# Projections as three one-pass products of split operands, values as a sixth strip, x-hat normalised on GpSimd

## The chip, the cores and the metric

One core of a Trainium2 chip. The metric is the device time of one launch in microseconds (us). The core's engines run side by side and meet through semaphores: TensorE (PE; its weight loads are shown apart as PEld), VectorE (DVE), ScalarE (ACT), GpSimd (POOL), and SyncE (SP), which issues most DMAs.

## The reference

x is 2 x 2048 tokens of 512 features. One block of attention with a memory term, then a feed-forward product in rounded float8:

```python
x = L0_attn_x
xh = layernorm(x)                                  # no scale, no shift
q = xh @ Wq.T; k = xh @ Wk.T; v = xh @ Wv.T        # 512, 128 and 128 columns
# 4 query groups x 8 heads of 16; 8 heads of keys and values
probs = softmax(einsum('bsqhd,bthd->bqhst', qh, kh) * scale)
a_dot = einsum('bqhst,bthd->bsqhd', probs, vh)
sigma_q = elu(q by groups of 128)
a_mem = sigma_q @ memory / (sigma_q @ memory_norm)
w = sigmoid(memory_weight)
x = x + a_dot * (1 - w) + a_mem * w
y = layernorm(x) / s, clipped and rounded to float8_e4m3, times s
return x + y @ (weight * weight_scale).T
```

## The kernel before

The program has a preparation and then 64 heads (8 chunks of 512 tokens x 8 heads; head n is chunk n // 8). The change touches the preparation, and a little of the step into the first head.

*Preparation.* It runs over 8 chunks of 512 tokens (NG). For each chunk x-hat is made and turned so that features lie on partitions: VectorE's `statistics` (L1077, bn_stats) and `mean_and_variance` (L1082), GpSimd's `rstd_of` (L546, L549: an addition and a power of -1/2 on 128 x 4), VectorE's `normalise` (L1089, four 128 x 512 operations from resid to xn), TensorE's `turn_xn` (L743: for each of four k, four fp32 transposes into a PSUM bank, two banks by turns), ScalarE's `copy_xnT` (L627). Then TensorE projects in five strips of 128 outputs by 512 tokens, four of queries and one of keys (`project`, L770: four fp32 products over k, into one of four PSUM banks by turns), and the values token by token (`project_v`, L782: 16 products with x-hat as the weights and 128 columns, all in one bank), which ScalarE copies into v_tiles (`copy_v`, L657).

*What becomes of a strip.* It is cut into three bf16 parts that sum to it: ScalarE's `first_part` (L633), VectorE's `rest` (L1205, in place in PSUM), ScalarE's `second_part` (L646), VectorE's `last_part` (L1113). Of queries, elu(q) goes to DRAM: ScalarE's Relu and Exp (`exp_neg`, L637 and L641), VectorE's `add_sigma` (L1193). GpSimd squares the first part (L579); TensorE sums squares by head (`query_norms` L751, `key_norms` L758, one product of an fp32r operand with ones); VectorE keeps the largest (`largest_norm`, L1117). Keys are also summed (`sum_keys`, L1199). A bank is free for the strip four further on when its last part is written (part3_ready).

*The guard.* From the norms of a batch (chunks 0 to 3, 4 to 7) VectorE computes a bound on the scores (`guard_sums` to `fill_guard_rows`, L1143 to L1187), in chunk 4 for the first batch and behind chunk 7 for the second; if it is too wide, a slow path is taken (it isn't here). For the second batch the chain is VectorE, TensorE (L762), VectorE, GpSimd's root (L554), VectorE, TensorE's transpose (L832), VectorE's maximum and comparison (L1260, L1262), and a register load on TensorE.

*Order.* Each engine's program is written out by hand, in the order in which it works; nothing plans it. In a chunk TensorE has strips 0 to 4 (the key norms of the chunk before after strip 0), turns k = 0, 1 of the next chunk, query norms, values, turns k = 2, 3. VectorE, for each strip o: add_sigma(o), rest(o), last_part(o - 1), with the normalisation of the next chunk after strip 2, then statistics two chunks on. ScalarE, for each strip: first_part, exp_neg, second_part(o - 1). GpSimd: the squares, and rstd before strip 2's. SyncE stores 4 sigma strips and 15 parts a chunk, loads x two chunks on, stores v, in chunks 5 and behind 7 the guard's rows too, and in chunk 6 loads the first head's operands.

*Heads.* Head 0 begins when TensorE has scored two units (`score_early_units`, L850) and ScalarE exponentiates them (L707); TensorE weighs the values (L910). 64 heads follow.

Of the kernel before, what the change touches and what calls it, by code (L numbers as in the profile page):

```python
# [77 lines left out]

EXP_UNIT = 4 * math.log(2)
# [22 lines left out]
def attention_ffn(nc, x, Wq, Wk, Wv, memory, memory_norm, memory_weight, weight, weight_scale, input_scale, out,  # L102
# [5 lines left out]
    with ExitStack() as ctx:  # L108
# [13 lines left out]
        head_ones_r = sb("head_ones_r", [P, P], F32R)  # L122
# [6 lines left out]
        wT_ffn = sb("wT_ffn", [P, KT, DM], BF16)  # L129
# [7 lines left out]
        pool = sb("pool", [P, 8192], F32)  # L137
        probs = pool[:, 0:RING * QG * CH].rearrange("p (a b) -> p a b", a=RING)
        late_probs = pool[:, RING * QG * CH:(RING + 1) * QG * CH]
        by_token = sb("by_token", [P, QG, TPC, VW], F32)  # L140
        rden = sb("rden", [P, QG, TPC], F32)
        head_out = sb("head_out", [P, QG, TPC, DH], F32)

        xnT = pool[:, 0:4096].rearrange("p (a k s) -> p a k s", a=2, k=KT)
        xn = pool[:, 4096:6144].rearrange("p (t d) -> p t d", t=TPC)

        wqT = sb("wqT", [P, KT, DM], F32)
        wkT = sb("wkT", [P, KT, KV], F32)
        wvT = sb("wvT", [P, KT, KV], F32)
# [3 lines left out]
        k_sq = sb("k_sq", [P, CH], F32R)  # L153
        v_tiles = sb("v_tiles", [P, 2, HEADS, TPC, VW], F32)

        work = sb("work", [P, 8, CH], F32)
        late = work[:, :, :].rearrange("p a s -> p (a s)")
        late_x, late_z, late_p = (late[:, i * LATE * CH:(i + 1) * LATE * CH] for i in range(3))
        tile_work = [parts[:, :, :, :].rearrange("p o i s -> p (o i s)")[:, i * 2 * CH:(i + 1) * 2 * CH].bitcast(F32) for i in range(3)]
        neg, epos = work[:, 0:2, :], work[:, 2:4, :]  # L160
# [3 lines left out]
        sigma_st = wqT[:, 0, :]  # L164
# [3 lines left out]
        w_val = sb("w_val", [P, KT, DM], BF16)  # L168
        xqT = sb("xqT", [P, KT, P], BF16)
        xq_now = sb("xq_now", [P, DM], BF16)  # L170

        last_probs = pool[:, 0:RING * QG * CH].rearrange("p (a x q s) -> p a x q s", a=LAST_RING, x=2, q=QG)
        last_by_token = by_token[:, :, :, :].rearrange("p q t v -> p (q t v)").rearrange("p (t q v) -> p t q v", t=TPC, q=QG)
        last_xqT = pool[:, 0:TPC * KT * P // 2].bitcast(BF16).rearrange("p (t k s) -> p t k s", t=TPC, k=KT)
# [19 lines left out]
        gm_space = wkT[:, :, :].rearrange("p k o -> p (k o)").bitcast(BF16)[0:QG * TPC, :]  # L194
# [5 lines left out]
        pj = [ps[:, i, :] for i in (2, 3, 5, 6)]  # L200
# [10 lines left out]
        v_bank = [vp] * (NG - 2) + [tp[1], vp]  # L211
# [21 lines left out]
        w_copied = sem("w_copied")  # L233
        dec = sem("dec")
# [9 lines left out]
        xnT_ready = sem("xnT_ready")  # L244
# [13 lines left out]
        v_proj_ready = sem("v_proj_ready")  # L258
# [56 lines left out]
        def _(sp):  # L315
# [32 lines left out]
            def store_parts(c, par):  # L348
# [9 lines left out]
                for o in range(QG + 1):  # L358
# [15 lines left out]
                    if c == NG - 1 and o == QG - 1:  # L374
                        sp.wait_ge(sigma_stored[0], 32)
                        sp.wait_ge(proj_ready, c * (QG + 1) + QG)
                        load_sigma(0)
                if c < NG - 2:
                    store_v(c, par)
                elif c == NG - 1:  # L380
                    store_v(NG - 2, 1 - par)
                    store_v(NG - 1, par)
# [67 lines left out]
            for par in range(2):  # L450
                sp.wait_ge(v_stored[par], 16 * (NG // 2 + 1))
# [23 lines left out]


# [42 lines left out]
        def _(pool_e):  # L519
# [31 lines left out]

            def bound_roots(b):
# [28 lines left out]
            pool_e.tensor_tensor(head_ones_r[:, :], head_ones[:, :], head_ones[:, :], ALU.mult)  # L581
# [17 lines left out]
        def _(act):  # L599
# [4 lines left out]
            act.sem_inc(xnT_ready, TWO_FREE)  # L604
# [17 lines left out]
            def copy_xnT(c, par, ks, first=False):  # L622
                if not first:
                    act.wait_ge(v_proj_ready, c)
# [842 lines left out]
```

## Time and profile before

| | us |
|---|---|
| median of 3 runs | 2044.28 (2043.74 to 2045.47) |
| the profiled execution, its own time | 2043.78 |
| its span, first to last instruction | 2042.1 |
| first strip of chunk 1 starts | 37.48 |
| first strip of chunk 7 starts | 172.52 |
| first exponential of head 0 in the chain | 201.38 |

The span is what the trace covers, and the execution's own time has 1.7 us around it. The preparation is the first tenth of the span. A row of the chain of waits gives when a piece starts, how long it holds the chain, and what it is; records of instructions in a timeline start a little earlier than in the chain and overlap, since matmuls are pipelined, so lengths of runs of matmuls are read from the chain. The granted TensorE clock is 1.00 in every stretch of the preparation, the full 2.4 GHz.

### The profile page before, as it was taken

The numbers are of one execution on the slowest core, as the hardware profiler recorded it, in microseconds if no ns is written. First come the engines' busy times: TensorE is split into PE (matmuls) and PEld (weight loads), VectorE is DVE, ScalarE is ACT, GpSimd is POOL, SyncE is SP. The second block draws the span as 40 slices with busy tenths as digits, with TensorE's granted clock in tenths as the row PEclk, the third lists the DMA queues.
The fourth block names the chain that finished last, engine by engine and source line by source line (L and its number), as shares of the span: only waits on it lengthen the run. The fifth ranks groups of instructions, "written<-read, shape, count | busy, mean of one in ns | idle before, by whom it ended". The sixth has DMA issues, their size and how long they took to land.

```text
span 2042.1 us, 63426 instructions
## 1 busy us (share of the span) xinstructions
PE 2029.6 (99%) x27795; PEld 900.6 (44%) x27796; DVE 1110.6 (54%) x1721; ACT 1934.1 (95%) x2183; POOL 79.7 (4%) x139
## 2 busy tenths in 40 slices
PE   9999999999999999999999999999999999999998
PEld 5555434444444444444444444444444444444445
DVE  5775555455545555455554555545554555545555
ACT  5555999999999999999999999999999999999997
POOL 3222000000000000000000000000000000000000
PEclk9999999999999999999999999999999999999999
DMA  5665311111211211112121211111121211121111
GB/s 199 197 195 170 90 49 49 39 34 49 51 51 35 67 51 52 48 44 55 50 51 41 61 51 51 51 53 43 49 51 51 57 45 51 51 68 30 49 50 46
DMA packets 137687, 131.68 MB, mean 64 GB/s; under 512 B 31619, under 2 KB 113947, under 8 KB 137435
## 3 DMA queue, kind: packets, MB, share of 16 engines
q1 hardware_dynamic: 136571, 126.25, 22.2%
q8 instruction: 219, 3.59, 0.8%
q10 hardware_dynamic: 864, 1.57, 0.2%
q14 instruction: 33, 0.27, 0.0%
HBM read 86.57 MB, written 37.49 MB: 61 GB/s over the span
## 4 chain that ended last, share of the span: by engine, by line
PE 98%; DVE 1%; DMA 0%; ACT 0%; issue 0%; ACTq 0%; POOL 0%; DVEq 0%
PE ps L850 43%; PE ps L910 43%; PE ps L770 7%; PE ps L950 1%; PE ps L782 1%; PE ps L934 1%; PE ps L743 1%; PE ps L1003 1%; PE ps L1020 1%; DMA y_out<-in_Wq 0%; PE ps L732 0%; PE ps L751 0%; PE ps L758 0%; ACT pool L707 0%; ACTq L601 0%
## 5 line engine op out<-in xcount | busy, mean ns | idle before, releaser
L707 ACT ACTIVATE pool<-ps 128x1024 f32<-128x1024 f32 x1953 | 1794.9, 1155 | 3.4 <-PE ps L850 0.7
L850 PE MATMUL ps<-q_st,k_st 99*32 99x512 bf16 x16128 | 1100.4, 379 | 0.8 <-PE ps L850 0.4
L910 PE MATMUL ps<-pool,v_st 128*32 128x512 f32 (+1 forms) x8568 | 1061.2, 567 | 0.0
L850 PEld LDWEIGHTS ps<-q_st,k_st 99*32 99x32 bf16 x16128 | 446.5, 96 | 805.2 <-issue 495.0
L910 PEld LDWEIGHTS ps<-pool,v_st 128*32 128x32 f32 x8568 | 273.8, 110 | 205.2
L1311 DVE STREAM_TRANSPOSE by_token<-ps 128x512 f32<-128x512 f32 x63 | 45.2, 717 | 476.7 <-PE ps L910 476.7
L1304 DVE SCALAR_TENSOR_TENSOR work<-work 128x1024 f32<-128x1024 f32 x189 | 231.5, 1225 | 6.5
L1290 DVE TENSOR_SCALAR work<-ps 128x512 f32<-128x512 f32 x126 | 87.1, 692 | 127.9 <-PE ps L850 127.9
L770 PE MATMUL ps<-pool,wqT 128*128 128x512 f32 x256 | 113.6, 594 | 0.4 <-ACT pool L627 0.3
L1367 DVE SCALAR_TENSOR_TENSOR y_out<-ps,scalars,resid 128x512 f32 (+1 forms) x28 | 21.0, 750 | 112.7 <-PE ps L934 112.7
L1295 DVE SCALAR_TENSOR_TENSOR work<-work 128x1024 f32<-128x1024 f32 x63 | 77.2, 1226 | 2.2
L1306 DVE SCALAR_TENSOR_TENSOR pool<-work 128x1024 f32<-128x1024 f32 x63 | 77.2, 1225 | 2.2
L633 ACT ACTIVATE parts<-ps 128x512 bf16<-128x512 f32 x40 | 23.9, 597 | 56.5 <-PE ps L770 56.5
L592 POOL TENSOR_TENSOR var_eps<-moments,eps 128x1 f32<-128x1 f32 x32 | 6.1, 190 | 1810.2 <-DVE moments L1340 1810.2
L1301 DVE SCALAR_TENSOR_TENSOR work<-work 128x1024 f32<-128x1024 f32 x63 | 76.7, 1217 | 0.0
L770 PEld LDWEIGHTS ps<-pool,wqT 128*128 128x128 f32 x256 | 47.4, 190 | 54.5 <-issue 51.5
L1193 DVE SCALAR_TENSOR_TENSOR y_out<-work,ps 128x512 f32<-128x512 f32 x32 | 21.9, 683 | 48.8 <-ACT work L641 48.8
L1378 DVE SCALAR_TENSOR_TENSOR resid<-ps,rnorm,resid 128x128 f32 (+1 forms) x128 | 39.0, 346 | 15.1 <-DVE rnorm L1374 14.6
L1299 DVE TENSOR_SCALAR work<-work 128x1024 int32<-128x1024 int32 x63 | 43.7, 694 | 2.2
L1292 DVE TENSOR_SCALAR work<-work 128x1024 f32<-128x1024 f32 x63 | 43.7, 694 | 2.1
L934 PE MATMUL ps<-wT_ffn,xqT 128*32 128x512 bf16 x448 | 44.5, 380 | 0.0
L950 PE MATMUL ps<-mem_aug,wqT 128*32 128x129 f32 x1024 | 39.7, 273 | 0.0
(131 smaller groups left out, 842.8 us busy)
## 6 DMA issues: line engine op xcount, KB each, us to landing
q_st<-q_aug SPq DMA_DIRECT2D x384, 64.0 KB
v_st<-v_aug SPq DMA_DIRECT2D x64, 256.0 KB
q_aug<-parts SPq DMA_DIRECT2D x96, 128.0 KB
k_st<-k_aug SPq DMA_DIRECT2D x64, 192.0 KB
sigma_kept<-y_out SPq DMA_DIRECT2D x32, 256.0 KB, 3.9
k_st<-k_aug SPq DMA_DIRECT2D x64, 128.0 KB
wqT<-sigma_kept SPq DMA_DIRECT2D x32, 256.0 KB, 3.2
resid<-in_x SPq DMA_DIRECT2D x7, 1024.0 KB, 9.0
```

The lines of the kernel that those rows point to most:

```text
L707: act.activation(held[:, half_u * 2 * CH:half_u * 2 * CH + 2 * CH], sc[unit % SLOTS].rearrange("p a b -> p (a b)"), ACT.Exp, scale=EXP_UNIT)\
L770: last = pe.matmul(pj[i % len(pj)], w, xnT[:, par, k, :], start=(k == 0), stop=(k == KT - 1))
L850: last = pe.matmul(dst[VW * c:VW * c + VW, :], k_st[0:AUG, par, keys:keys + VW], q_st[0:AUG, par, q * CH:q * CH + CH], start=True, stop=True)
L910: last = pe.matmul(acc[par][VW * c:VW * c + VW, :].rearrange("v (i s) -> v i s", s=VW)[:, places, :], v_st[:, par, j, :], by_place[:, c, p ...
L934: last = pe.matmul(ffn_ps[VW * c:VW * c + VW, :], xqT[:, k, VW * c:VW * c + VW], wT_ffn[:, k, :], start=(k == 0), stop=(k == KT - 1))
L950: last = pe.matmul(am[VW * c:VW * c + VW, t, :], sigma_st[:, tokens:tokens + VW], mem_aug[:, :], start=True, stop=True)
L1290: dve.tensor_scalar(late_x[:, d * CH:d * CH + CH], acc[1 - par], LOWEST, None, ALU.max).then_inc(late_taken, 1)
L1295: dve.scalar_tensor_tensor(late_x, late_z, ROUND, late_x, ALU.subtract, ALU.subtract).then_inc(late_step, 1)
L1301: dve.scalar_tensor_tensor(late_p, late_x, POWER[4], late_x, ALU.add, ALU.mult).then_inc(late_step, 1)
L1304: dve.scalar_tensor_tensor(late_p, late_p, POWER[i], late_x, ALU.add, ALU.mult).then_inc(late_step, 1)
L1306: dve.scalar_tensor_tensor(late_probs[:, LATE * CH:2 * LATE * CH], late_p, POWER[0], late_z, ALU.add, ALU.mult)\
L1311: dve.transpose(by_token[:, :, :, :].rearrange("p q t v -> p (q t v)"), acc[par]).then_inc(acc_read, 1)
```

## The change

The operands of the projections are each written as two fp32r tiles, a high part (what a ScalarE copy into fp32r keeps) and a low part (VectorE: the turned value less the high part). Each fp32 product over k becomes three one-pass products: high weight by high x-hat, low weight by high x-hat, high weight by low x-hat (PASSES). The same splitting is done once for the turned weights (`split_weight`), which lie in other PSUM banks than before (WEIGHT_BANK).

The values are projected like a query strip, as strip 5 of the chunk, into the ring of four banks; ScalarE copies them to v_turn (`take_v`), and TensorE turns them back by tokens with four transposes (`turn_v`) behind the first strip of the next chunk; `copy_v` follows there. For chunk 7 the turning stands behind the two early units of head 0 and its copy behind ScalarE's second exponential. Chunk 6's and chunk 7's value strips both stand in the last chunk, as before.

The normalisation of chunks 1 to 7 moves from VectorE to GpSimd, before the squares of the chunk ahead of it; that of chunk 0 stays on VectorE. TensorE turns k = 0, 1 of the next chunk behind strip 2 and k = 2, 3 behind strip 3 (in chunk 0 behind strips 3 and 4). The turning of k = 2 waits until the low part of k = 0 is written, since both use one bank. The squares of keys are bf16 rather than fp32r. SyncE stores a chunk's values one chunk later. Tiles of the preparation and of the heads share space by the order of allocation.

```diff
+PASSES = ((0, 0), (1, 0), (0, 1))
+V_STRIP = QG + 1
+STRIPS = [(c, o) for c in range(NG) for o in range(QG + 1 + (c < NG - 2))] + [(NG - 2, V_STRIP), (NG - 1, V_STRIP)]
+STRIP_NUMBER = {co: s for s, co in enumerate(STRIPS)}
+WEIGHT_BANK = (5, 4, 2, 3, 0, 1)
+FIRST_TURN_BANK = (6, 7, 0, 1)
+LAST_V_AT = 1
+TURN_AFTER = (3, 2)
...
+            x_high = early("x_high", [P, 2, KT, CH], F32R)
+            x_low = early("x_low", [P, 2, KT, CH], F32R)
+            xn = early("xn", [P, TPC, DM], F32)
...
+            wq_low = early("wq_low", [P, KT, DM], F32R)
+            wk_low = early("wk_low", [P, KT, KV], F32R)
+            wv_low = early("wv_low", [P, KT, KV], F32R)
+            v_turn = early("v_turn", [P, CH], F32)
...
+        def bank(c, o):
+            return pj[STRIP_NUMBER[c, o] % len(pj)]
+
+        def turn_bank(c, k):
+            return ps[:, FIRST_TURN_BANK[k], :] if c == 0 else tp[k % 2]
+
+        v_bank = [vp] * (NG - 1) + [n2]
...
+                    if o == 0 and 0 < c < NG - 1:
+                        store_v(c - 1, 1 - par)
+                if c == NG - 1:
                     store_v(NG - 2, 1 - par)
-                    store_v(NG - 1, par)
...
+            def normalise(c, par):
+                pool_e.wait_ge(rstd_ready, c + 1)
+                pool_e.wait_ge(tp_ready, c * KT)
+                for t in range(TPC):
+                    last = pool_e.tensor_scalar(xn[:, t, :], resid[:, c * TPC + t, :], moments[:, par, t, 0:1],
+                                                rstd[:, par, t:t + 1], ALU.subtract, ALU.mult)
+                last.then_inc(xn_ready, 1)
...
-                    if o == 2 and not last:
-                        pool_e.wait_ge(sq_ready, c * (QG + 1) + o)
+                    if o == 0 and not last:
                         rstd_of(c + 1, 1 - par)
-                        pool_e.wait_ge(rstd_ready, c + 2)
+                        normalise(c + 1, 1 - par)
...
+            def copy_x_high(c, par, ks):
+                if c >= 2:
+                    act.wait_ge(proj_ready, STRIP_NUMBER[c - 2, V_STRIP] + 1)
                 for k in ks:
                     act.wait_ge(tp_ready, c * KT + k + 1)
-                    act.activation(xnT[:, par, k, :], tp[k % 2], ACT.Copy).then_inc(xnT_ready, 1)
+                    act.activation(x_high[:, par, k, :], turn_bank(c, k), ACT.Copy).then_inc(x_high_ready, 1)
...
+            def take_v(c):
+                act.wait_ge(proj_ready, STRIP_NUMBER[c, V_STRIP] + 1)
+                act.wait_ge(v_turned, c)
+                act.activation(v_turn[:, :], bank(c, V_STRIP), ACT.Copy).then_inc(v_taken, 1)
...
                         second_part(c, o - 1)
+                    elif c == 0:
+                        for j in (KT, KT + 1):
+                            copy_weight(j)
+                        act.wait_ge(small_loaded, 80)
+                        act.activation(e_neg, mem_w, ACT.Exp, scale=-1.0).then_inc(e_neg_ready, 1)
+                    else:
+                        copy_v(c - 1, 1 - par)
+                    if o == TURN_AFTER[c > 0]:
+                        copy_x_high(c + 1, 1 - par, range(KT // 2))
+                    elif o == TURN_AFTER[c > 0] + 1:
+                        copy_x_high(c + 1, 1 - par, range(KT // 2, KT))
+                second_part(c, QG)
                 if c < NG - 2:
...
+                    take_v(c)
...
+                    if unit == LAST_V_AT:
+                        copy_v(NG - 1, (NG - 1) % 2)
...
-                    pe.wait_ge(xnT_ready, c * KT + k + 1)
+                    if c > 0:
+                        pe.wait_ge(x_low_ready, c * KT + max(k - 1, 0))
                     for t in range(TPC):
-                        last = pe.transpose(tp[k % 2][:, t * P:t * P + P], xn[:, t, k * P:k * P + P], ident[:, :])
+                        last = pe.transpose(turn_bank(c, k)[:, t * P:t * P + P], xn[:, t, k * P:k * P + P], ident[:, :])
...
+            def product(c, par, o, k, p):
+                w_part, x_part = PASSES[p]
+                if o < QG:
+                    w = (wqT, wq_low)[w_part][:, k, o * P:o * P + P]
+                else:
+                    w = ((wkT, wk_low), (wvT, wv_low))[o - QG][w_part][:, k, :]
+                return pe.matmul(bank(c, o), w, (x_high, x_low)[x_part][:, par, k, :],
+                                 start=(k == 0 and p == 0), stop=(k == KT - 1 and p == len(PASSES) - 1))
+
+            def bank_free(c, o):
+                s = STRIP_NUMBER[c, o]
+                if s < len(pj):
+                    if s == 1:
+                        pe.wait_ge(x_low_ready, 1)
+                    return
+                held_c, held_o = STRIPS[s - len(pj)]
+                if held_o == V_STRIP:
+                    pe.wait_ge(v_taken, held_c + 1)
+                else:
+                    pe.wait_ge(part3_ready, held_c * (QG + 1) + held_o + 1)
+
+            def project(c, par, o, ks=range(KT)):
                 for k in ks:
-                    if o == 0:
-                        pe.wait_ge(xnT_ready, c * KT + k + 1 + TWO_FREE)
-                    w = wqT[:, k, o * P:o * P + P] if o < QG else wkT[:, k, :]
-                    last = pe.matmul(pj[i % len(pj)], w, xnT[:, par, k, :], start=(k == 0), stop=(k == KT - 1))
+                    for p in range(len(PASSES)):
...
+            def first_of_chunk(c, par):
                 for k in range(KT):
...
+                    pe.wait_ge(x_high_ready, c * KT + k + 1)
+                    for p in range(2):
+                        product(c, par, 0, k, p)
+                for k in range(KT):
+                    pe.wait_ge(x_low_ready, c * KT + k + 1)
+                    last = product(c, par, 0, k, 2)
+                last.then_inc(proj_ready, 1)
+
+            def turn_v(c):
+                pe.wait_ge(v_taken, c + 1)
+                if c < NG - 1:
+                    pe.wait_ge(v_tile_ready, c + ONE_FREE)
+                for t in range(TPC):
+                    last = pe.transpose(v_bank[c][:, t * P:t * P + P], v_turn[:, t * P:t * P + P], ident[:, :])
+                last.then_inc(v_turned, 1)
 
             def chunk(c, par, first_guard=False):
                 for o in range(QG + 1):
...
+                    bank_free(c, o)
+                    if c == 0:
+                        pe.wait_ge(w_split, o + 1)
+                    if o == 0:
+                        first_of_chunk(c, par)
+                    else:
+                        project(c, par, o)
+                    if o == 0:
+                        if c == 0:
+                            for j in (KT, KT + 1):
+                                turn_weight(j)
+                        else:
+                            key_norms(c - 1)
+                            turn_v(c - 1)
                     if first_guard and o == 2:
                         pe.wait_ge(v_tile_ready, c + 1)
                         mean_key_norm(0)
-                turn_xn(c + 1, range(KT // 2))
+                    if c == 0 and o == TURN_AFTER[0]:
+                        pe.wait_ge(w_split, KT + 2)
+                    if o == TURN_AFTER[c > 0]:
+                        turn_xn(c + 1, range(KT // 2))
+                    elif o == TURN_AFTER[c > 0] + 1:
+                        turn_xn(c + 1, range(KT // 2, KT))
                 query_norms(c)
-                if first_guard:
-                    pe.wait_ge(bound_in, 2)
                 if c < NG - 2:
-                    pe.wait_ge(v_tile_ready, c + 1)
-                    for t in range(TPC):
-                        project_v(c, par, t)
-                    turn_xn(c + 1, range(KT // 2, KT))
+                    bank_free(c, V_STRIP)
+                    if c == 0:
+                        pe.wait_ge(w_split, KT + 2)
+                    project(c, par, V_STRIP)
...
+            def split_weight(j):
+                dve.wait_ge(w_copied, j + 1)
+                turned = ps[:, WEIGHT_BANK[j], :]
+                if j < KT:
+                    high, low = (w[:, :, j * P:j * P + P] for w in (wqT, wq_low))
+                    dve.tensor_tensor(low, turned.rearrange("p (k o) -> p k o", k=KT), high.bitcast(F32), ALU.subtract)\
+                        .then_inc(w_split, 1)
+                else:
+                    high, low = (w[:, :, :].rearrange("p k o -> p (k o)") for w in ((wkT, wk_low), (wvT, wv_low))[j - KT])
+                    dve.scalar_tensor_tensor(low, turned, SCALE / EXP_UNIT if j == KT else 1.0, high.bitcast(F32),
+                                             ALU.mult, ALU.subtract).then_inc(w_split, 1)
+
+            def split_x(c, par, k):
+                dve.wait_ge(x_high_ready, c * KT + k + 1)
+                dve.tensor_tensor(x_low[:, par, k, :], turn_bank(c, k), x_high[:, par, k, :].bitcast(F32), ALU.subtract)\
+                    .then_inc(x_low_ready, 1)
 
             statistics(0)
             dve.wait_ge(stats_ready, 1)
             mean_and_variance(0)
...
+            split_weight(0)
+            normalise_first()
+            split_weight(1)
+            for k in range(KT // 2):
+                split_x(0, 0, k)
+            split_weight(2)
+            split_x(0, 0, 2)
+            split_weight(3)
+            split_x(0, 0, 3)
+            dve.wait_ge(x_loaded[1], 16)
+            statistics(1)
...
+                dve.wait_ge(stats_ready, c + 2)
+                mean_and_variance(1 - par)
                 for o in range(QG + 1):
+                    if o == TURN_AFTER[c > 0] + 1:
+                        for k in range(KT // 2):
+                            split_x(c + 1, 1 - par, k)
+                    elif o == TURN_AFTER[c > 0] + 2:
+                        for k in range(KT // 2, KT):
+                            split_x(c + 1, 1 - par, k)
                     if o < QG:
```

## Rows read from the trace of the kernel before

**Rows 1.** The page, busy time: us, share of the span, instructions.
```profile
PE 2029.6 (99%) x27795; PEld 900.6 (44%) x27796; DVE 1110.6 (54%) x1721; ACT 1934.1 (95%) x2183; POOL 79.7 (4%) x139
```
**Rows 2.** Busy time by stretch, chunk 1: stretch, length, engines' us (instructions), clock, DMA.
```profile
40.90:64.20 23.30, 23.30 (x95) 13.23 (x94) 15.81 (x29) 12.76 (x24) 6.40 (x7) 1.00 0.61 197
```
**Rows 3.** Chain of waits: start us, us, what (instructions).
```profile
37.48 3.44 PE ps L770 x8
...
41.14 13.73 PE ps L770 x32
54.88 0.87 PE ps L743 x8
55.75 0.33 PE ps L751 x4
56.08 3.77 PE ps L782 x32
...
60.72 3.44 PE ps L770 x8
64.16 0.24 PE ps L758
...
153.84 3.44 PE ps L770 x8
...
172.52 1.10 PE ps L770 x2
...
201.38 1.91 ACT pool L707 x2
```
**Rows 4.** Groups by shape, 0 to 170 us: busy us, mean ns | idle before.
```profile
L782 PEld LDWEIGHTS ps<-wvT,pool 128*128 128x128 f32 x192 | 21.9, 192 | 1.4 <-issue 1.4
L770 PEld LDWEIGHTS ps<-pool,wkT 128*128 128x128 f32 x55 | 10.4, 190 | 13.2 <-issue 13.2
L579 POOL TENSOR_TENSOR q_sq<-parts 128x512 bf16<-128x512 bf16 x28 | 29.3, 1045 | 83.2 <-ACT parts L633 82.6
L540 POOL MEMSET ones_row<- 128x512 bf16 x1 | 0.6, 550 | 0.0
```
**Rows 5.** Timeline of ScalarE in chunk 4, one strip: start us, us, instruction.
```profile
117.81 0.60 ACT L633 ACTIVATE parts<-ps 128x512 bf16<-128x512 f32 x1 [1.14 <-PE ps L770]
118.30 0.59 ACT L637 ACTIVATE work<-ps 128x512 f32<-128x512 f32 x1
118.98 0.63 ACT L641 ACTIVATE work<-work 128x512 f32<-128x512 f32 x1
119.52 0.58 ACT L646 ACTIVATE parts<-ps 128x512 bf16<-128x512 f32 x1
```
**Rows 6.** Timeline of VectorE in chunk 4.
```profile
116.21 0.69 DVE L1193 SCALAR_TENSOR_TENSOR y_out<-work,ps 128x512 f32<-128x512 f32 x1 [1.28 <-ACT work L641]
116.82 0.69 DVE L1205 TENSOR_TENSOR ps<-ps,parts 128x512 f32<-128x512 f32 x1
...
125.86 0.65 DVE L1160 TENSOR_TENSOR bound<-bound 128x1 f32<-128x1 f32 x1
...
128.58 0.68 DVE L1199 TENSOR_REDUCE k_sum<-ps 128x1 f32<-128x512 f32 x1
...
131.74 2.46 DVE L1077 BATCH_NORM_STATS2 stats<-resid 128x6 f32<-128x512 f32 x4
```
**Rows 7.** Timeline of GpSimd in chunk 4: the two steps of rstd.
```profile
118.53 0.20 POOL L546 TENSOR_TENSOR var_eps<-moments,eps 128x4 f32<-128x4 f32 x1 [2.44 <-DVE moments L1082]
118.81 1.01 POOL L549 TENSOR_TENSOR rstd<-var_eps,minus_half 128x4 f32<-128x4 f32 x1
```
**Rows 8.** Chain of waits in chunk 0, at the first turning of x-hat.
```profile
10.76 0.21 issue
10.97 0.64 PE ps L743 x4
```
**Rows 9.** Timeline of VectorE in chunk 0: its four normalisations, merged.
```profile
8.96 1.91 DVE L1089 TENSOR_SCALAR pool<-resid,moments,rstd 128x512 f32<-128x512 f32 x4 [1.42 <-POOL rstd L549]
```

More of the change, by code:

```diff
@@ L474, in _ @@
                 sp.wait_ge(gm_loaded, 16 * QK_LOADS * (NG * HEADS + 1) + 32)
+            store_v(NG - 1, 1)
+            for par in range(2):
+                sp.wait_ge(v_stored[par], 16 * (NG // 2 + 1))
             def load_block(g, h):
@@ L686, in last_chunk @@
                         second_part(c, o - 1)
+                take_v(c - 1)
+                second_part(c, QG)
                 copy_v(c - 1, 1 - par)
-                second_part(c, QG)
-                copy_v(c, par)
-            copy_xnT(0, 0, range(KT), first=True)
-            for j in (KT, KT + 1):
-                copy_weight(j)
-            act.wait_ge(small_loaded, 80)
-            act.activation(e_neg, mem_w, ACT.Exp, scale=-1.0).then_inc(e_neg_ready, 1)
+                take_v(c)
+            copy_x_high(0, 0, range(KT))
             for c in range(NG - 1):
@@ L766, in project @@
                 for k in ks:
-                    if o == 0:
-                        pe.wait_ge(xnT_ready, c * KT + k + 1 + TWO_FREE)
-                    w = wqT[:, k, o * P:o * P + P] if o < QG else wkT[:, k, :]
-                    last = pe.matmul(pj[i % len(pj)], w, xnT[:, par, k, :], start=(k == 0), stop=(k == KT - 1))
+                    for p in range(len(PASSES)):
+                        last = product(c, par, o, k, p)
                 if KT - 1 in ks:
                     last.then_inc(proj_ready, 1)
-            def project_and_turn(c, par):
-                for k in range(KT // 2):
-                    project(c, par, 0, range(k, k + 1))
-                    turn_xn(c, range(KT // 2 + k, KT // 2 + k + 1))
-                project(c, par, 0, range(KT // 2, KT))
@@ L833, in last_chunk @@
                 last.then_inc(ranges_ready, 1)
-                for t in range(1, TPC):
-                    project_v(c, par, t)
-            pe.wait_ge(w_copied, 2)
-            turn_xn(0, range(KT // 2))
-            pe.wait_ge(w_copied, KT)
-            project_and_turn(0, 0)
-            for j in (KT, KT + 1):
-                turn_weight(j)
+            turn_xn(0, range(KT))
             for c in range(NG - 1):
@@ L1112, in last_part @@
                 dve.wait_ge(part2_ready, i + 1)
[L1113 removed]
+                dve.tensor_tensor(parts[:, o, 2, :], bank(c, o), parts[:, o, 1, :], ALU.subtract).then_inc(part3_ready, 1)
             def largest_norm(c, of_keys):
@@ L1217, in chunk @@
                         largest_norm(c - 1, 1)
-                    if o == 1:
-                        dve.wait_ge(stats_ready, c + 2)
-                        mean_and_variance(1 - par)
+                    if c == 0 and o == 0:
+                        for j in (KT, KT + 1):
+                            split_weight(j)
+                        weights_of_memory()
                     if first_guard:
@@ L1229, in chunk @@
                             fill_guard_rows(0)
-                    if o == 2:
-                        normalise(c + 1, 1 - par)
                 last_part(c, QG)
+                if c == 0:
+                    for k in range(KT // 2, KT):
+                        split_x(c + 1, 1 - par, k)
                 largest_norm(c, 0)
```

203 lines of the change are left out of this document (85 added, 118 removed).

## The prediction

> **What bounds the kernel now.** I read the page first: TensorE is busy 99% of the span [rows 1], so only an edit that shortens TensorE's own queue, or starves it, can move the time. The diff touches only the preparation (eight chunks of 512 tokens, before the attention heads). The busy time by stretch [rows 2] shows that in one chunk of 23.3 us TensorE works for all of it, VectorE 15.8, ScalarE 12.8, GpSimd 6.4. The chain of waits [rows 3] gives the chunk by pieces: the first strip of chunk 1 starts at 37.48 and that of chunk 2 at 60.72, a period of 23.25 us with nothing but TensorE in it: five strips of 3.44 (1 x 3.44 at 37.48, 4 at 41.14 in 13.73; 8 instructions each, so 0.859 per product of 128 x 512), two turnings of x-hat at 0.87, query norms 0.33, key norms 0.23, values 3.77. Chunk 6 leaves its values for later (153.84 to 172.52, 18.7 us), and from the first strip of chunk 7 to the first exponential of head 0 (201.38) it is 28.9 us. After that TensorE and ScalarE are both nearly full for 1840 us in code that the diff leaves alone.
>
> **The products.** An fp32 product is two instructions of 0.429; a one-pass fp32r product is not in the projections now, but the key norms are one: 0.24 in the chain at 64.16 [rows 3] for 512 columns. Three passes in place of one fp32 product cost between 3 x 0.2147 = 0.644 (a quarter of 0.859 is one pass) and 3 x 0.235 = 0.705. I take the first: the key norms stand alone between other kinds, each change of kind paying a little, while these are 12 alike in a row. Each pass brings its own weight load, shown 190 ns long [rows 4]; the load hides if it can run beside the pass before. The values' products show it can: 32 loads of 192 ns with 32 instructions in 3.77 us, one every 0.118 [rows 3, 4], well under 0.2147. A strip is then 12 x 0.2147 = 2.58 (upper end 2.82).
>
> **The values** become a sixth strip, 2.58, and four transposes back, half of a turning of 0.87, 0.44: 3.02 for 3.77. TensorE's own work in a chunk becomes 6 x 2.58 + 2 x 0.87 + 0.44 + 0.33 + 0.22 = 18.2 for 23.25. Taking the strip out costs ScalarE one more pass of 0.5 (start to start, [rows 5]); its load goes 12.8 to about 13.5, no bound.
>
> **VectorE** loses four normalisations and gains four subtractions of the high part (like its line 1205, 0.60 from start to start, [rows 6]). 25 such operations are 15.0, with aggregation 15.4 in 18.2: little room, and its order matters. I walk one steady chunk, 0 being the start of strip 0, with the steps in the program's order. TensorE: strip 0 to 2.58, key norms and values back to 3.24, strip 1 to 5.82, strip 2 to 8.40, x-hat k = 0, 1 turned to 9.27, strip 3 to 11.85. The turning of k = 2 needs its bank, which frees when the low part of k = 0 is written. ScalarE on strip 2: first part 8.44, Relu +0.49, Exp +0.68, done at 10.24; it copies the two high parts by about 11.8. VectorE: sigma of strip 2 at 10.3, rest 10.9, last part of strip 1 at 11.5, low part of k = 0 at 12.1 to 12.8, of k = 1 to 13.4. TensorE answers a release about 0.4 late (four transposes after a wait took 0.21 + 0.64, not 0.44: [rows 8]), so k = 2, 3 are turned by 14.1, not 12.72. **This new wait of about 1.4 us a chunk** is the dearest thing that the change adds. Strip 4 ends 16.7, norms 17.0, values 19.6. Period 19.6, a gain of 3.65.
>
> **GpSimd** takes the four normalisations (128 x 512, fp32, one tensor input, two operations). No row has this form. Below: the fill of ones_row, 0.55; above: a two-input product of the same size takes 1.04 [rows 4], and if both operations cost a pass each over its fixed 0.2, 0.2 + 2 x 0.84 = 1.9. I take 1.04, the nearest row in size and kind. What hangs on it: the loop from the end of strip 4, e. VectorE: key sums e + 0.7, rest, two last parts, query norm, four statistics (2.4, [rows 6]) and aggregation give moments at e + 6.7; GpSimd's rstd +1.35 [rows 7]; four normalisations; TensorE's 0.4, turning, strip 3, turning, strip 4: +7.3. Loop 15.4 + 4X: 19.55 at X = 1.04, level with the other wait; so dearer normalisations are paid at once, 4X a chunk, and cheaper ones gain nothing in a steady chunk. GpSimd's queue behind them (squares 0 to 3) is caught up by 13.7, before the query norms at 16.7. The other things moved cost nothing: SyncE's stores of a chunk issue in about 13 to 18 us and are wanted a chunk later; the x load for two chunks on is issued in the first microseconds and wanted at 20.
>
> Here the Trainium skill can be weighed. "Trainium Architecture — The Big Picture" (section "The five engines, in one table") says that streaming elementwise work is twice as slow on GpSimd as on VectorE; "GPSIMD Engine Reference", section 3.1, says that bodies of one or two operations run at 1.03 cycles an element, only two-input ones at 2.6. Doubling VectorE's fastest (an estimate, 2 x 0.53) gives about the 1.04 above and the sum below; the other rule gives, as an estimate, about 0.6, and 1.5 us less in the guard chunk. No row settles it, and neither rule gives a new rival.
>
> **Chunk 0.** First weights are copied as now, VectorE splits weight 0, then normalises (1.91 us now, from 8.96, [rows 9]) by 11.0. High parts come every 0.5 from 11.7; VectorE, which also splits weights 1 to 3 between, ends the last low part at 16.0, so strip 0 ends 16.3 (17.0 now). Weights K and V are turned by 17.2, strips 1 to 3 end 19.8, 22.4, 25.0; turning to 25.9, strip 4 to 28.4, then the wait for the low parts to 30.6, norms and values: chunk 1 starts at 33.5, not 37.48: gain 4.0.
>
> **Chunk 4** computes the guard on VectorE: 2.7 us from 125.86 to 128.58 [rows 6], now ahead of the low parts of k = 2, 3. It keeps its 19.6, but moments of the next chunk come 2.5 late, so chunk 5 turns k = 0, 1 only at 6.15 + 1.35 + 4.16 + 0.4 = 12.1, and lasts 21.6. **Chunk 6** is 19.6 - 2.6 = 17.0. **Chunk 7**: strips 0 to 3 end at 10.5; strip 4 and its norms 13.5; half of V6, then key norms wait for VectorE's largest query norm to 15.1; V6 ends 16.6, V7 with the turning of V6 19.95, ranges 20.2; then VectorE's maximum and comparison, a register load on TensorE and the first unit's scores, an estimate of 2 for all (none of it is exposed now): first exponential at about 22.3, now 28.9. The last copy of values, so far ahead of the first exponential, now stands behind the second: 0.6 on a ScalarE that is nearly full.
>
> **Sum.** First exponential at 33.5 + 4 x 19.6 + 21.6 + 17.0 + 22.3 = 172.8, now 201.4: gain 28.6, less 0.6: 28.0. The profiled execution took 2043.8 (span 2042.1), the median is 0.5 above it: 2015.8, and 2016 against the median of 2044.3.
>
> **Ends.** No wait at all for low parts, and a cheap normalisation: 6 x 1.4 + 2 less: 2006. Passes at 0.235: 0.24 a strip, 48 strips, some of it absorbed by the waits: +10, 2026. Normalisation at 1.9: loop 23.0, +3.4 in six chunks, near +20: 2036.
>
> **Rivals.**
> (A) VectorE's wait is not there, because the low parts come earlier than I walk, and TensorE alone sets the chunk: 18.2, time 2006. For: 2.8 us of VectorE's room; against: the order of its queue, written down, puts three operations ahead.
> (B) The normalisation on GpSimd becomes the bound, at 1.3 to 2.2 us each: each of six chunks is longer by 4X - 4.2, which gives 2022 to 2044, at 1.9 2036. For: GpSimd's power of four elements takes 1.0 [rows 7], so some of its forms are dear; against: its product of 512 takes 1.04 with two inputs.
> (C) The other side, one mechanism: the same place, the four normalisations between moments and turning, at 2.7 each (three passes of 0.84 and 0.2). Loop 26.2 in place of 19.6, six chunks, +40 on the forecast: 2056. It decides from 2.2 us each on, where the loop is 24.3 and the 28 us gained are spent over six chunks.
> (D) The load isn't hidden behind a single pass: 0.19 + 0.21 each, strip 4.8, chunk 31.7, about 2105. Against it stand the values' loads, one in 0.118.
> (E) It doesn't do what it says: a product called one-pass streams its four-byte elements at half rate, 0.43 each. Strip 5.2, chunk 34, about 2120; the key norms' 0.24 speak against it.
>
> **Numbers.** Forecast with its ends of the pass price 0.66, A 0.12, B 0.14, C 0.04, D with E 0.02, some other hold-up that eats the gain 0.02. A measurement of this kernel tells about 0.2% (4 us) from no change. Faster: 0.66 + 0.12 + most of B = 0.91; within: 0.03; slower 0.06. The range, 2007 to 2030, takes A's edge in and leaves out B's upper half, C and D.
>
> **What would show it.** Right: products of 0.215 in the chain, strips every 2.6; chunk starts 19.6 apart; in each chunk a wait of TensorE's transposes (turn_xn) on VectorE's split_x, about 1.4; GpSimd's normalisation near 1.0; first exponential near 173. Wrong if the transposes wait on GpSimd instead for several us (B or C), if the strips take over 3 us (D or E), if chunk starts are 18.2 apart (A), or if the 64 heads change their 28.7 us each (1840 over 64).

## The result, and the profile after

| | before | after |
|---|---|---|
| median, us | 2044.87 | 2064.74 (2063.64 to 2066.21, 4 runs) |
| ratio | | 1.0098, 95% interval 1.0081 to 1.0116 |
| span | 2042.1 | 2064.5 |
| first exponential of head 0 in the chain | 201.4 | 223.0 |
| from there to the end of the span | 1840.7 | 1841.5 |
| mean granted clock | 1.00 | 0.989 |

The change makes the kernel 20 us slower; 28 us faster was forecast. All of it lies in the preparation; the heads cost 0.8 more. The page after, busy time (us, share, instructions) and the group of GpSimd's normalisation (busy, mean ns | idle before), against [rows 1] and the 1.04 of the forecast:

```profile
PE 2016.5 (98%) x27828; PEld 972.8 (47%) x27828; DVE 1117.6 (54%) x1731; ACT 1938.5 (94%) x2191; POOL 136.0 (7%) x166
L585 POOL TENSOR_SCALAR xn<-resid,moments,rstd 128x512 f32<-128x512 f32 x28 | 57.7, 2075 | 0.7
```

TensorE is busy 13 us less, though part of its work ran at a lower clock, and in the preparation it no longer sets the time. One normalisation takes 2.07 us, all 28 of them within 2071 to 2083 ns. Who waited for whom from 0 to 200 us (total, times, longest):

```profile
PE ps L785 <- POOL xn L585: 30.4, 6, 6.1
```

A seventh stands in the same view without a releaser: in chunk 0 TensorE waits 3.4 us and turns at 29.17, when GpSimd's first four (20.81 to 29.07) are out.

The chain of waits after, from one turning of k = 0, 1 to the next (start, us, what; against [rows 3], where a chunk is nothing but TensorE):

```profile
52.27 1.97 PE ps L785 x8
54.24 4.32 PE ps L812 x12
58.58 0.60 ACT parts L667
...
62.31 1.20 DVE x_low L1177 x2
...
66.67 2.39 DVE stats L1148 x4
...
69.81 1.03 POOL rstd L578
...
73.01 2.01 POOL xn L585
75.07 4.14 POOL xn L585 x2
79.25 1.97 PE ps L785 x8
```

This is a closed loop of 27.0 us (each link waits for the one before it, and the first for the last): the turning, strip 3, ScalarE, VectorE's queue down to the statistics, rstd, four normalisations of 8.25 in all, and the turning again. All links but the first two are other engines' work. The first two, TensorE's, are themselves slow: eight transposes take 1.97 where they took 0.87, and 12 passes 4.32 where others in this trace take 2.75. The busy time by stretch, just behind the wait and a little later (stretch, length, engines, clock, DMA share, GB/s), against the 1.00 of [rows 2], says why:

```profile
53.00:58.00 5.00, 5.00 (x17) 4.13 (x16) 1.38 (x2) 1.19 (x2) 2.22 (x3) 0.55 0.71 235
58.60:64.40 5.80, 5.80 (x33) 4.46 (x32) 3.98 (x7) 4.25 (x8) 2.08 (x2) 1.00 0.07 17
```

Behind the idle stretch the granted clock is mostly at its lower level, 1.2 GHz, and returns to 2.4 GHz later.

### The profile page after: what moved, and what is told of

The parts are those of the page before. It is cut to its first block, busy times and chain, and to the rows that moved or that the text cites. A ratio compares the mean times of both kernels' runs of the same rounds, so it can differ in the third digit from the quotient of the medians.

```text
span 2064.5 us, 63537 instructions
## 1 busy us (share of the span) xinstructions
PE 2016.5 (98%) x27828; PEld 972.8 (47%) x27828; DVE 1117.6 (54%) x1731; ACT 1938.5 (94%) x2191; POOL 136.0 (7%) x166
## 3 DMA queue, kind: packets, MB, share of 16 engines
q10 hardware_dynamic: 864, 1.57, 0.2%
## 4 chain that ended last, share of the span: by engine, by line
PE 92%; DVE 3%; POOL 2%; issue 1%; ACT 1%; POOLq 0%; DVEq 0%; ACTq 0%; PEldq 0%
PE ps L920 42%; PE ps L981 42%; PE ps L812 3%; POOL xn L585 2%; PE ps L1021 1%; PE ps L1005 1%; PE ps L785 1%; DVE stats L1148 1%; PE ps L1074 1%; PE ps L1091 1%; DVE x_low L1177 0%; DVE parts L1210 0%; POOL rstd L578 0%; DVE ps L1302 0%; ACT parts L680 0%
## 5 line engine op out<-in xcount | busy, mean ns | idle before, releaser
L920 PEld LDWEIGHTS ps<-q_st,k_st 99*32 99x32 bf16 x16128 | 470.8, 96 | 782.5 <-issue 470.9
L1409 DVE SCALAR_TENSOR_TENSOR late<-late 128x1024 f32<-128x1024 f32 x189 | 231.6, 1225 | 6.5
L1395 DVE TENSOR_SCALAR late<-ps 128x512 f32<-128x512 f32 x126 | 87.2, 692 | 127.6 <-PE ps L920 127.6
L1411 DVE SCALAR_TENSOR_TENSOR pool<-late 128x1024 f32<-128x1024 f32 x63 | 77.2, 1226 | 2.2
L1400 DVE SCALAR_TENSOR_TENSOR late<-late 128x1024 f32<-128x1024 f32 x63 | 77.2, 1226 | 2.1
L1406 DVE SCALAR_TENSOR_TENSOR late<-late 128x1024 f32<-128x1024 f32 x63 | 76.7, 1218 | 0.0
L585 POOL TENSOR_SCALAR xn<-resid,moments,rstd 128x512 f32<-128x512 f32 x28 | 57.7, 2075 | 0.7
L785 PE MATMUL ps<-ident,xn 128*128 128x128 f32 x128 | 22.1, 331 | 35.2 <-POOL xn L585 30.4
L812 PE MATMUL ps<-x_high,wqT 128*128 128x512 f32 x128 | 55.7, 435 | 0.0
L812 PE MATMUL ps<-x_high,wq_low 128*128 128x512 f32 x128 | 53.4, 417 | 0.0
L812 PE MATMUL ps<-x_low,wqT 128*128 128x512 f32 x128 | 49.6, 417 | 0.6 <-DVE x_low L1177 0.6
L1290 DVE SCALAR_TENSOR_TENSOR y_out<-epos,ps 128x512 f32<-128x512 f32 x32 | 21.9, 685 | 49.5 <-ACT epos L675 49.5
```

The costliest lines, as they stand in the source:

```text
L585: last = pool_e.tensor_scalar(xn[:, t, :], resid[:, c * TPC + t, :], moments[:, par, t, 0:1], rstd[:, par, t:t + 1], ALU.subtract, ALU.mult)
L812: return pe.matmul(bank(c, o), w, (x_high, x_low)[x_part][:, par, k, :], start=(k == 0 and p == 0), stop=(k == KT - 1 and p == len(PASSES) ...
L920: last = pe.matmul(dst[VW * c:VW * c + VW, :], k_st[0:AUG, par, keys:keys + VW], q_st[0:AUG, par, q * CH:q * CH + CH], start=True, stop=True)
L1395: dve.tensor_scalar(late_x[:, d * CH:d * CH + CH], acc[1 - par], LOWEST, None, ALU.max).then_inc(late_taken, 1)
L1400: dve.scalar_tensor_tensor(late_x, late_z, ROUND, late_x, ALU.subtract, ALU.subtract).then_inc(late_step, 1)
L1406: dve.scalar_tensor_tensor(late_p, late_x, POWER[4], late_x, ALU.add, ALU.mult).then_inc(late_step, 1)
```

## The experiments

Each is a change to the changed kernel, unless it says otherwise. Ratios are against the kernel before.

**e1: all four normalisations on VectorE.**

```diff
-                        normalise(c + 1, 1 - par)          # GpSimd, strip 0
...
+                    if o == 0:
+                        normalise_dve(c + 1, 1 - par)      # VectorE, behind rest(c, 0)
```

> The changed kernel with the four normalisations of a chunk back on VectorE (behind the rest of strip 0, before sigma of strip 1); rstd stays on GpSimd, everything else of the change stays. Theory G (GpSimd's 2.07 us for each normalisation, in a loop moments - normalisation - turning - strip 3 - VectorE's queue - statistics, is what lengthens the chunk from 23.3 to 27.1 us): without it a chunk is TensorE's 19.2 plus about 1.5 of the wait for the low parts, near 21, the granted clock is back at 1.00, and the time is near 2028. Rival V (VectorE's queue with four subtractions more is the bound, and GpSimd only hides it): VectorE gets 2.4 us more a chunk, chunks stay at 25 or more, and the time is 2055 or higher.

Measured 2030.67, ratio 0.9938 (0.9921 to 0.9954). This one edit takes 34.1 us off and turns the loss into a gain, with the clock at 1.00. Rival V falls. In the chain, the values of one chunk with strip 0 of the next come every 20.65 us:

```profile
55.68 5.68 PE ps L811 x24
...
76.33 5.68 PE ps L811 x24
```

Its waits (engine, line, total, times, longest) hold the one that the forecast called the dearest, at less than it said (1.3 once, in chunk 0, and 0.42 or 0.43 in each chunk behind it, for 1.4), and ScalarE's timeline shows one that it did not have, in chunk 7:

```profile
PE ps L784 <- DVE x_low L1184: 3.9, 7, 1.3
PE ps L784 <- DVE xn L1166: 2.3, 5, 1.2
```
```profile
168.31 0.60 ACT L666 ACTIVATE parts<-ps 128x512 bf16<-128x512 f32 x1 [2.19 <-DMA q_aug<-parts]
```

**e2: the same work, taken earlier.**

```diff
+                    if o == 3 and c + 2 < NG:
...
+                        statistics(c + 2)
...
+                        mean_and_variance(par)             # was at the start of chunk c + 1
...
-                if c + 2 < NG:                             # behind largest_norm(c, 0)
-                    statistics(c + 2)
```

> The changed kernel with the normalisation still on GpSimd, but statistics and moments of the chunk after next taken earlier: in VectorE's queue behind strip 3's work, not behind the chunk's last part and query norm. Nothing is made cheaper. Theory G, as a loop: GpSimd can start some 8 us sooner, its 2.07 each is covered, chunks fall to 20.5 to 22, time 2026 to 2034, with L585 still at 2.07. Rival P (the price itself counts, GpSimd's 14.8 us a chunk in its own queue with the squares): chunks 24 or more, 2048 or more.

Measured 2034.11, ratio 0.9952 (0.9935 to 0.9968), with the normalisation still at 2.08 each. Nothing was made cheaper, and 30.6 us went. So it isn't the price by itself but the price inside a closed loop: P falls, and GpSimd's 14.8 us a chunk fit in one of 20.9. What remains is TensorE's wait for low parts (5.7 us over seven chunks) and a new one behind VectorE's query norm, which the statistics delay (4.8 us in all).

**e3: the kernel before, with the move alone.**

```diff
                         rstd_of(c + 1, 1 - par)
-                        pool_e.wait_ge(rstd_ready, c + 2)
+                        normalise(c + 1, 1 - par)          # GpSimd
...
-                    if o == 2:                             # VectorE
-                        normalise(c + 1, 1 - par)
```

> The kernel before with one part of the change alone: the four normalisations moved from VectorE (behind strip 2) to GpSimd (behind rstd, where that stands now). Theory G: moments come at 11 us of a chunk of 23.25, rstd to 12.3, normalisation to 20.6, the turning is due at 17.4, and the squares of three strips stand behind it too: 4 to 6 us lost in each of seven chunks, 2072 to 2086. Rival (the move costs only because the chunk became shorter than GpSimd's work; the longer chunk hides it): 2044 to 2050. The duration of one normalisation: 2.07 if it is the instruction's own, less if VectorE's and GpSimd's work at the same places made it slow.

Measured 2089.66, ratio 1.0228 (1.0211 to 1.0245): 45 us lost, 3.7 more than the upper end. The move is a loss in the long chunk too, and the same wait and the same slow pieces behind it show it:

```profile
PE ps L751 <- POOL pool L556: 25.8, 7, 4.2
```
```profile
65.75 1.97 PE ps L751 x8
67.72 0.03 issue
67.76 0.62 PE ps L759 x4
68.37 4.12 PE ps L790 x32
```

The transposes at 1.97 again, the values at 4.12 for 3.77 [rows 3]: 1.7 us in this chunk (with the query norms at 0.62 for 0.33) to the slower clock, which my expectation had not counted. In four of the other five chunks with values in this place they take 5.07 to 5.62 in the chain; an estimate from these rows is 17 us in all, beside the 25.8 of the wait. The price is 2.07 here too.

**e4: what the price is made of.**

```diff
-                for t in range(TPC):
...
+                pool_e.tensor_scalar(xn[:, 0, :], resid[:, c * TPC, :], moments[:, par, 0, 0:1],
+                                     rstd[:, par, 0:1], ALU.subtract, ALU.mult)
+                pool_e.tensor_scalar(xn[:, 1, :], resid[:, c * TPC + 1, :], moments[:, par, 1, 0:1], None, ALU.subtract)
+                pool_e.tensor_scalar(xn[:, 2, :], resid[:, c * TPC + 2, :], 0.0, 1.0, ALU.subtract, ALU.mult)
+                pool_e.tensor_scalar(xn[:, 3, :], resid[:, c * TPC + 3, :], 1.0, None, ALU.mult).then_inc(xn_ready, 1)
```

> The changed kernel with GpSimd's four normalisations in four forms, to read the price of each from the trace: tile 0 as it is (two operations, both operands by pointer), tile 1 the subtraction alone by pointer, tile 2 two operations with constants, tile 3 one operation with a constant. It leaves out rstd, or all of the normalisation, in tiles 1 to 3; x has mean near 0 and spread near 1, so that the work behind is the same. If each operation costs a pass: 2.07, near 1.1, 2.07, near 1.1. If the pointers cost: 2.07, 1.5 to 2.07, near 1.1, near 1.1. If it is a fixed price of the instruction or of its contention: 2.07 for all. With the saving of 2 to 3 us in each chunk's loop the time is 2045 to 2053.

One run, 2054.49, 1.5 above the range expected. Groups by shape (busy, mean ns | idle before); the lines in the order of the tiles are 584, 586, 587, 588:

```profile
L584 POOL TENSOR_SCALAR xn<-resid,moments,rstd 128x512 f32<-128x512 f32 x7 | 14.6, 2090 | 0.8
L587 POOL TENSOR_SCALAR xn<-resid 128x512 f32<-128x512 f32 x7 | 13.5, 1931 | 0.0
L586 POOL TENSOR_SCALAR xn<-resid,moments 128x512 f32<-128x512 f32 x7 | 11.0, 1570 | 0.0
L588 POOL TENSOR_SCALAR xn<-resid 128x512 f32<-128x512 f32 x7 | 10.5, 1501 | 0.0
```

None of the three readings holds. The instruction costs 1.50 with one operation and a constant; the second operation adds 0.43 to 0.52, the pointers 0.07 to 0.16. The barest form is dearer than the two-input product at 1.04 [rows 4], which I had taken for the nearest row. That product is bf16 and these are fp32, so the type and the instruction are not told apart here.

**e5: TensorE kept busy in the wait.**

```diff
             def turn_xn(c, ks):
+                if c > 0 and 0 in ks:
+                    for i in range(40):
+                        pe.transpose(tp[0][:, 0:P], ident[:, :], ident[:, :])
                 pe.wait_ge(xn_ready, c + 1)
```

> The changed kernel, with 40 transposes of the identity into the idle turning bank (4.4 us at the full clock) put into TensorE's queue ahead of each wait for xn; nothing else moves. In the changed kernel the eight transposes behind the wait take 1.97 us in the chain and not 0.87, strip 3 takes 4.3 to 4.6 and not 2.75, and the granted clock of such stretches is 0.83. If that slower clock is a part of the loss: 2.3 to 2.8 us back in each of six chunks, time 2048 to 2052, chunks near 24.4. Rival (the queue of VectorE and the normalisation set the chunk whatever TensorE's clock): 2062 to 2066, or more for the work put in.

Measured 2052.34, ratio 1.0040 (1.0026 to 1.0054): 12.4 us back for useless work. The chain from turning to turning, and the stretch of above:

```profile
52.09 1.09 PE ps L788 x8
53.19 2.78 PE ps L815 x12
...
76.69 1.09 PE ps L788 x8
```
```profile
53.00:58.00 5.00, 5.00 (x28) 4.22 (x27) 1.46 (x3) 2.85 (x6) 3.08 (x4) 1.00 0.64 221
```

24.6 a chunk, not 27.0, in the same loop, and the clock of the stretch is 1.00 where it was 0.55. The clock is a second cost of the wait, and on the path. By a rule of the Trainium skill ("TensorE: Matmul & The Clock Gate", "The HAM clock gate") the gate takes the array to 1.2 GHz when it idles, and activity opens it again; the rows at 0.55 (behind the wait) and 1.00 (the wait filled with work) agree, and e5 gives its price here.

**e6: two of the four on each engine.**

```diff
-                for t in range(TPC):          # GpSimd
+                for t in range(2, TPC):       # tiles 0 and 1 on VectorE, in the place of e1's four
```

> The changed kernel with two of the four normalisations of a chunk on VectorE (behind the rest of strip 0) and two on GpSimd. Theory G: the loop falls by 2 x 2.07 = 4.15 us from 27.1 to 22.9, and with TensorE's wait shorter than before its clock stays up and 2.7 more goes, down to the floor of 20.7 to 21 that the kernel with all four on VectorE shows: 2028 to 2032. If the clock doesn't come back with the shorter wait: 22.9 a chunk, 2038 to 2042. Rival (any normalisation on GpSimd costs the same, by its order ahead of the squares): 2055 or more.

Measured 2027.32, ratio 0.9919 (0.9902 to 0.9935): the loop falls by 6.4 to 20.6 a chunk, near the 4.15 of two normalisations and the clock's 2.4 together. TensorE still waits for GpSimd, but 4.4 us in all and never over 2.0, and the clock stays at 1.00. It is better than all four on either engine.

**e7: the first head's operands loaded later** (on e1: `PREFETCH_FROM = CPB + 3`).

> The kernel of e1 (normalisation on VectorE) with SyncE's loads of the first head's operands (10 loads, some 6 us of its queue) moved from chunk 6 to chunk 7. In e1 ScalarE waited in chunk 7 for stores of chunk 6's parts that SyncE had issued late (2.2, 0.4 and 1.1 us). If SyncE's queue is on the path there: 3 to 5 us less than e1, 2026 to 2028. Rival (the wait only stands in place of another, or the loads then hold up the first head): within 1.5 us of e1's 2030.7, or later.

Measured 2038.03, ratio 0.9971 (0.9960 to 0.9981): a miss, 7.4 us slower than e1. ScalarE's wait in chunk 7 is gone (strips 0 and 1 of chunk 7 run 24 passes in 5.67, those behind them 33 in 7.52 without a break), but the load of v_st now stands in SyncE's queue behind the stores of strip 3, and head 0 waits for it:

```profile
187.13 3.53 DMA v_st<-v_aug
190.66 1.53 issue
192.19 1.90 PE ps L919 x16
```

**e8: k = 2, 3 turned behind strip 4** (on e7).

```diff
-                    elif o == TURN_AFTER[c > 0] + 1:       # TensorE and ScalarE
+                    elif o == QG:
...
-                    elif o == TURN_AFTER[c > 0] + 2:       # VectorE, ahead of strip 4's work
-                        for k in range(KT // 2, KT):
-                            split_x(c + 1, 1 - par, k)
...
-                if c == 0:                                 # VectorE, behind last_part(c, QG)
+                if c >= 0:
```

> The kernel of e7 with the turning of k = 2, 3 behind strip 4 instead of strip 3 (in chunks 1 to 6), and VectorE's low parts of k = 2, 3 behind the last part of strip 4. Forecast's step on the new wait: TensorE stands 1.0 to 1.4 us a chunk at the turning of k = 2, since the low part of k = 0 isn't out of VectorE's queue yet; with 5.5 us between the turnings it is gone, six chunks, 6 to 8 us less than e7: 2019 to 2021, chunks near 19.4. Rival A (VectorE is the bound and the wait comes back elsewhere): within 2 us of e7.

Measured 2034.92, ratio 0.9957 (0.9940 to 0.9974), 3.1 less than e7 where 6 to 8 were expected. The wait for the low parts is gone in chunks 1 to 6 and the turnings of k = 0, 1 come at 66.00 and 85.90, 19.9 apart for 20.65. That is 0.75 a chunk and not the 1.0 to 1.4 of my expectation, since the wait had been 3.9 us over seven chunks in all (e1 and e7 alike). The wait for VectorE's fourth normalisation is 2.3 us in all, as it was in e7; a wait for head 0's operands 1.4 longer (10.9 for 9.5) takes back some of the rest.

**e9: all ten loads together, behind strip 0's stores of chunk 7** (on e8), and **e10: one of the four normalisations on GpSimd** (on e9).

> The kernel of e8 (normalisation on VectorE, turning of k = 2, 3 behind strip 4) with all ten loads of the first head's operands issued together behind strip 0's stores of chunk 7. In e8 head 0 began 10.9 us late, because the load of v_st stood in SyncE's queue behind the stores of strip 3 of chunk 7. If SyncE's queue was all of it: the 10.9 us go but for some 1 us, 2023 to 2026. Rival (the stores of chunk 7 that now come later, or the loads' own landing, hold head 0 or 1 up instead): 2030 or more.

> The kernel of e9 with one of the four normalisations of a chunk on GpSimd (2.07, in time beside VectorE's three). In e8 the turning of k = 0, 1 waited for VectorE's fourth normalisation by 0.5 us a chunk, with periods of 19.9. If GpSimd's one is covered (moments 1.35 + 2.07 before VectorE's three are out): 19.4 a chunk, 2 to 3 us less than e9. Rival (the GpSimd normalisation comes last and sets the turning): the same as e9 within 1, or slower.

e9: 2025.93, ratio 0.9908 (0.9891 to 0.9924): 9.0 of the 10.9 are back, so SyncE's queue was it. e10: 2023.68, ratio 0.9899 (0.9883 to 0.9916), 2.3 less than e9, the fastest: 21 us under the kernel before, 41 under the change. From turning to turning in e10 it is 19.6 once, behind VectorE's normalisation, and then 19.4, with nothing but TensorE in the chain:

```profile
47.09 1.09 PE ps L783 x8
48.19 5.48 PE ps L810 x24
...
66.71 0.88 PE ps L783 x8
67.58 5.46 PE ps L810 x24
73.04 0.87 PE ps L783 x8
73.92 0.33 PE ps L791 x4
74.25 5.66 PE ps L810 x24
...
86.08 0.88 PE ps L783 x8
```

What still holds VectorE's normalisation up shows in e1's timelines of the two engines. One of its four takes 1.34 beside GpSimd's square, where the others take 0.54:

```profile
65.49 1.34 DVE L1166 TENSOR_SCALAR xn<-resid,moments,rstd 128x512 f32<-128x512 f32 x1
65.50 1.04 POOL L614 TENSOR_TENSOR q_sq<-parts 128x512 bf16<-128x512 bf16 x1 [1.07 <-ACT parts L666]
```

In e6, with two normalisations on each engine, VectorE's take 0.89 (median of 14) and GpSimd's 2.09; in e10 GpSimd's one takes 2.33 (median of 7). These are slow when both engines work at once; no run tests why.

## Why the prediction was wrong, step by step

**The step that failed: "I take 1.04, the nearest row in size and kind".** A normalisation on GpSimd takes 2.07, twice the term in the sum and above the upper end of 1.9 too. The row chosen was a tensor_tensor, whose two inputs seemed to make it the dearer form; e4 shows that a tensor_scalar costs 1.50 before its second operation. The two rules of the Trainium skill weighed there both fell short: twice VectorE's time ("Trainium Architecture — The Big Picture", "The five engines, in one table") against a measured 2.07 / 0.535, 3.9 times, and 1.03 cycles an element for a one-input body ("GPSIMD Engine Reference", 3.1), an estimate of 0.6. The measurement decides. The mechanism was on the table, as rivals B and C: at 2.07 mine gave a loop of 23.7 and some 2040, still a gain. That leaves two terms of the loop:

**"Loop 15.4 + 4X" was 0.9 short.** In e5, at the full clock, it is 24.6. It closes through strip 3 and VectorE's queue behind it (sigma, rest, last part, two low parts, key sums, rest), not through the end of strip 4.

**The clock was no term at all.** Between e5 and the change lie 12.4 us, 2.4 a loop. I took the pieces of the turning and of the strips at the durations of a TensorE that never stops; behind a wait of 4 to 6 us they took longer (1.97 for 0.87, 3.4 to 4.6 for 2.75). With both, and the 15 us below, the sign turns well below the 2.2 that I gave C. Two estimates: the 20 us lost are 3.3 a loop, so 1.2 us a normalisation if the clock stays as it was (2.07 - 3.3 / 4); the 8 us that e5 still loses are 1.3 a loop, so 1.7 with the clock up. e4, at a mean of 1.77 for its four forms, was still 10 us slower than the kernel before.

**How the 49 us between 2016 and 2065 divide.** 34 are GpSimd's normalisation (e1 against the change), 12.4 of them the clock (e5), the other 21.7 the loop. The other 15 are in e1 as well. Chunk 7's strip 0 starts at 161.3 there for a forecast 150.5, and from there to the first exponential it takes 25.2 for 22.3:

- *The price of a pass.* Forecast 0.2147, upper end 0.235; measured 5.48 / 24 = 0.228. Strips take 2.75, not 2.58: near 8 us over 48 strips, inside the range given. The weight load does hide (D falls) and a pass is a pass (E falls).
- *Chunk 0.* Forecast to gain 4.0; strip 0 of chunk 1 starts at 37.9 in e1 and 38.6 in the change, for 33.5 forecast and 37.5 before. In the change it is held by the 3.4 us wait for GpSimd; in e1 its chain is VectorE's queue, which I had walked too fast: weight parts, x-hat's low parts, statistics, the scalars' seven small operations.
- *"The other things moved cost nothing".* True of the change itself, false as soon as chunks take 20.6: ScalarE waited in chunk 7 for the landing of stores that SyncE had issued late (2.2, 0.4 and 1.1 us in e1). The ten loads are a cause (the wait goes with them in e7); the guard's rows stand in the same queue, and their part was not tested. Moving the loads costs more or less by where they are put (e7, e9).

**Right:** TensorE's own work a chunk, but for the dearer pass (18.2 forecast, 19.4 in e10, where nothing else is in the chain); the register load on the path before head 0 (0.99 us of issue at 221.28, behind VectorE's comparison); 0.6 more in the heads (0.8).

**Half right:** the new wait for low parts. It is there once GpSimd is off the path (e1) and gone with e8, but costs 0.75 a chunk and not 1.4; in the change itself it doesn't show, because TensorE waits longer for GpSimd. Rival A (no such wait, TensorE alone sets the chunk) is false of the change and of e1, and true of e10's steady chunks.

The forecast with e1's placement would have been 15 us too low, and of the right sign.

**Open:** what in GpSimd's tensor_scalar takes the 1.50, the instruction or its fp32 type (the product at 1.04 is bf16), was not looked into. The normalisation as two tensor_tensor operations or on ScalarE was not tried, nor the change without the value strip.

## What to carry to other kernels

An operation that no row of the trace shows has no nearest row: another instruction on the same engine, of another type, was off by a factor of two here, in the direction that its operands spoke against, and 28 of them decided the sign. When work is moved to an idle engine, write down the loop that it closes (who starts it, who waits, and how that leads back to its start) before asking whether the engine has room: GpSimd was 7% busy over the span and still on the path of every chunk of the preparation but the last; from 20 to 220 us it was busy 53% of the time. With the same work issued 8 us sooner, or halved, the kernel was within 4 us of the one with all of it on VectorE (2034.1 and 2027.3 for 2030.7). And a wait on TensorE behind which its clock is lower, as behind those of 4 to 6 us here, is paid twice.

## What the runs showed of the hardware that I had not expected

- GpSimd, 128 x 512 fp32 tensor_scalar: 2.07 to 2.09 with two operations by pointer, 1.93 with constants, 1.57 and 1.50 with one; a bf16 tensor_tensor of the size 1.04, VectorE's tensor_scalar 0.535 (e1, e4). Beside work on the other engine GpSimd's took up to 2.35 (e6, e10) and VectorE's up to 1.34 (e1).
- TensorE behind waits of 4 to 6 us: granted clock 0.55 over the next 5 us in the stretch shown, eight fp32 transposes 1.97 for 0.87 to 1.09, 12 passes 3.4 to 4.6 for 2.75. Behind waits of up to 2.0 us (e6) it stayed at 1.00. Forty useless transposes in the wait saved 12.4 us in six chunks.
- A one-pass fp32r product of 512 columns with its own weight load comes every 0.228 us in a stream of 24 (e10), an fp32 product every 0.859 [rows 3]: three passes cost 0.80 of it, where three quarters was forecast.
